# Deformable sampling and whitening on one core: an order of the stages by rounds, and a sampling step of short multiplies with one sum over the four corners

## The reference

```python
# layer 0, on n = group_norm(x, 32 groups)
offsets = conv3x3(n, offset_w) + offset_b          # 8 channels: (x, y) for 4 groups
mod     = 1 + tanh(conv3x3(n, mod_w) + mod_b)      # 4 channels
v       = conv1x1(n, kv_w)[256 value channels]     # 8 heads of 32
sampled = bilinear(v, pixel position + offsets) * mod   # 4 corners, weights times validity
x       = x + conv1x1(sampled, out_w) + out_b
# layer 1, on m = group_norm(x, 32 groups)
cov     = covariance of m over all images, in 16 groups of 16 channels, + 1e-4 I
x       = x + (cov ** -0.5) @ (m - mean) * weight + bias
```

## Time and profile before

| | us |
|---|---|
| median of three runs | 6920.73 |
| profiled execution, its own time | 6926.74 |
| its span, first to last instruction | 6925.0 |
| POOL busy | 4650.6 |
| PE busy | 4573.9 |
| DVE busy | 4258.7 |
| ACT busy | 1105.9 |
| mean granted TensorE clock | 0.833 |

### The profile page before, as it was taken

How to read it: one execution, slowest core, us unless ns; L and a number is a source line. 1 busy time by engine, 2 the same in 40 slices (tenths; PEclk the granted TensorE clock), 3 DMA queues, 4 the chain that set the end, 5 groups by cost and what they waited for, 6 DMA issues and landing times.

```text
span 6925.0 us, 71293 instructions
## 1 busy us (share of the span) xinstructions
PE 4573.9 (66%) x17916; PEld 2997.6 (43%) x17916; DVE 4258.7 (61%) x8374; ACT 1105.9 (16%) x2723; POOL 4650.6 (67%) x4115
## 2 busy tenths in 40 slices
PE   5866666666667666666666666666666544447777
PEld 3544444444444444444444444444444333334222
DVE  6766666666666666666666666666655544445555
ACT  1211112111211121112111121112111111110000
POOL 0277777777777777777777777777777777760000
PEclk9988888888888888888888888888888766668999
DMA  8966667666666667667676676676666544446999
GB/s 269 297 227 230 223 224 234 230 222 232 230 225 226 227 221 234 225 230 231 224 232 224 219 235 232 224 234 200 214 198 210 159 136 137 136 153 251 421 421 416
DMA packets 1069691, 1612.55 MB, mean 233 GB/s; under 512 B 92080, under 2 KB 617008, under 8 KB 1067568
## 3 DMA queue, kind: packets, MB, share of 16 engines
q0 software_dynamic: 196608, 537.13, 24.2%
q10 hardware_dynamic: 632832, 536.91, 23.1%
q1 hardware_dynamic: 240176, 537.77, 21.3%
HBM read 1074.58 MB, written 536.87 MB: 233 GB/s over the span
## 4 chain that ended last, share of the span: by engine, by line
POOL 66%; issue 19%; DMA 9%; PE 3%; DVE 2%; POOLq 0%; ACT 0%; DVEq 0%; ACTq 0%; SPq 0%
POOL patch L836 66%; DMA out_dram<-vring 4%; DMA vring<-x 3%; DMA v<-vring 1%; PE psT L1088 1%; PE psA L937 0%; DVE vring L782 0%; PE psG L1088 0%; PE psI L1088 0%; PE psO L937 0%; DVE bst L406 0%; PE psI L952 0%; PE psA L890 0%; DVE vring L472 0%; PE psT L894 0%
## 5 line engine op out<-in xcount | busy, mean ns | idle before, releaser
L836 POOL DMA_INDIRECT patch<-v,index_now x4096 | 4644.7, 1134 | 1537.4 <-issue 1536.8
L566 DVE TENSOR_TENSOR patch<-patch,weight 128x2048 f32<-128x2048 f32 x512 | 1173.0, 2291 | 1988.4 <-DMA patch<-v,index_now 1936.1
L937 PE MATMUL psA<-wB,xa_mem 128*128 128x364 f32 x3824 | 1525.0, 540 | 65.1 <-DVE taps L484 57.6
L990 PE MATMUL psT<-ident,xr 128*128 128x128 f32 x2048 | 462.9, 402 | 1519.6 <-DVE xr L582 1508.9
L990 PEld LDWEIGHTS psT<-ident,xr 128*128 128x128 f32 x2048 | 373.4, 210 | 1724.0 <-DVE xr L582 1703.8
L937 PEld LDWEIGHTS psA<-wB,xa_mem 128*128 128x128 f32 x3824 | 801.9, 226 | 449.4 <-issue 137.7
L976 PE MATMUL psO<-sampT,wO_sb 128*128 128x512 f32 x2048 | 928.8, 596 | 0.9 <-ACT sampT L1123 0.9
L1140 ACT ACTIVATE x1T<-psT 128x512 f32<-128x512 f32 x512 | 302.2, 597 | 3179.4 <-PE psT L990 3169.2
L965 PE MATMUL psT<-ident,samp 128*128 128x128 f32 x2048 | 387.4, 317 | 467.2 <-DVE samp L573 460.8
L568 DVE TENSOR_TENSOR patch<-patch 128x1024 f32<-128x1024 f32 x512 | 627.1, 1225 | 17.5
L1005 PE MATMUL psG<-x1T 128*128 128x129 f32 x4096 | 614.0, 314 | 10.1 <-ACT x1T L1140 10.1
(11 more groups left out here) (197 smaller groups left out, 2839.3 us busy)
## 6 DMA issues: line engine op xcount, KB each, us to landing
v<-vring ACTq DMA_DIRECT2D x256, 1024.0 KB, 6.8
xa_mem<-x_dram SPq DMA_DIRECT2D x256, 512.0 KB, 8.4
xr<-x_dram SPq DMA_DIRECT2D x256, 512.0 KB, 6.4
x<-xr ACTq DMA_DIRECT2D x256, 512.0 KB, 3.0
xs_mem<-x_dram SPq DMA_DIRECT2D x224, 512.0 KB, 7.7
patch<-v,index_now POOLq DMA_INDIRECT x4096, 4.2
patch<-x SPq DMA_DIRECT2D x64, 1024.0 KB, 12.3
out_dram<-patch ACTq DMA_DIRECT2D x64, 1024.0 KB, 19.9
```

Of the source, the lines that this page charges most:

```text
L566: eng.tensor_tensor(v4, v4, w4, ALU.mult).then_inc(weighted, 1)
L836: eng.indirect_dma_start(out=patch[n][:, t, :], out_offset=None, in_=v2_flat[k], in_offset=bass.IndirectOffsetOnAxis(ap=index_now[n][:, t: ...
L937: mm = eng.matmul(conv_bank[wide][r][:, 0:NA], xa[j][:, c, r * W:(r + 1) * W], wB[:, c, :], start=(c == 0), stop=(c == CC - 1))
L990: mm = eng.transpose(psT[h][:, at:at + P], xr[j][:, c, row * W:(row + 1) * W], ident[:, :])
```

## The change

In VectorE's `sample` the one multiply of 2048 elements becomes four multiplies of 512 elements each (`SHORT` is 2 of the 8 image-row and group columns of a half), with one semaphore increment behind the fourth; the two adds become one `tensor_reduce` over the four corners, with the corner index as innermost axis. The `halved` semaphore goes.

The order of the round changes on every engine. VectorE: two rows of `conv_out`, both halves of `sample`, statistics, the other two rows, `place`, then the residual of the block before and, once per pair, the Gram sum of the pair before. TensorE: in round t it turns the samples of block t-1 instead of t, all four rows at once, and takes x1's turn and the Gram product of block t-2 instead of t-1; the output convolution stays at t-1, and moves from the front of the round to its end. ScalarE follows: `x1_store` and `x1_out` are of block t-2, `samples_out` is of block t-1. SyncE issues the load of the residual's x behind the statistics' load. The Gram sums are opened and closed within one pair (j = 0 opens, j = 1 closes), so that `gram_tail`, `gram_out` and the addition of the two (L665) are gone. At an image's end each engine works off the blocks that are left.

The diff, cut to its core (the same moves in ScalarE's `pair`, in the loads and in the semaphores' counts are left out):

```diff
+SHORT = 2
...
-                w4 = weight[:, bass.ds(((i * 2 + j) * 2 + h) * (NH * 4), NH * 4)].unsqueeze(2)\
-                    .to_broadcast([P, NH * 4, CG])
-                eng.tensor_tensor(v4, v4, w4, ALU.mult).then_inc(weighted, 1)
+                for t in range(0, NH, SHORT):
+                    w4 = weight[:, bass.ds((((i * 2 + j) * 2 + h) * NH + t) * 4, SHORT * 4)]\
+                        .unsqueeze(2).to_broadcast([P, SHORT * 4, CG])
+                    part = v4[:, t * 4:(t + SHORT) * 4, :]
+                    times = eng.tensor_tensor(part, part, w4, ALU.mult)
+                times.then_inc(weighted, 1)
                 eng.wait_ge(weighted, half)
-                eng.tensor_tensor(mine[:, :, 0:ENT], mine[:, :, 0:ENT], mine[:, :, ENT:PATCH],
-                                  ALU.add).then_inc(halved, 1)
-                eng.wait_ge(halved, half)
                 if h == 0:
                     eng.wait_ge(psT_free[CC - 1], (b * PAIRS + i) * 4 + 2 * j + SAMP_FREE - 3)
-                eng.tensor_tensor(samp[j][:, 2 * h:2 * h + 2, :].rearrange("p r (g e) -> p (r g) e", g=G),
-                                  mine[:, :, 0:CG], mine[:, :, CG:ENT], ALU.add)\
+                eng.tensor_reduce(samp[j][:, 2 * h:2 * h + 2, :].rearrange("p r (t e) -> p (r t) e", t=G),
+                                  mine.rearrange("p t (k e) -> p t e k", e=CG), AX_X, ALU.add)\
                    .then_inc(sampled[j][h], 1)
...
 # VectorE, pair
                     for j in range(2):
+                        if ca is not None and not (prepare and j == 0):
+                            conv_out(ca, ci, 1 - m, j, (0, 1), g is None)
                         if g is not None:
                             sample(g, i, m, q, j, 0)
-                            if j == 1:
-                                residual(g, i, 0)
-                            elif not first:
-                                residual(g, i - 1, 1)
-                                gram_add(g, i - 1)
+                            sample(g, i, m, q, j, 1)
...
+                        if g is not None:
+                            if j == 1:
+                                residual(g, i, 0)
+                                if not first:
+                                    gram_add(g, i - 1)
+                            elif not first:
+                                residual(g, i - 1, 1)
+                        if prepare and j == 0:
+                            prep(ca)
+                            conv_out(ca, ci, 1 - m, j, range(ROWS), g is None)
...
-            eng.wait_ge(psG_free, B * NG + 1)
-            step(eng.tensor_tensor(gram[:, :, :, :], gram[:, :, :, :], gram_tail[:, :, :, :],
-                                   ALU.add))
+            eng.wait_ge(psG_free, B * PAIRS + 1)
...
 # TensorE, pair
-                            conv((0, 1))
-                            before(out_conv)
-                            before(turn_x1)
-                            conv((2,))
+                            alongside = not (prepare and j == 0)
+                            if alongside:
+                                conv((0, 1))
+                            twice_before(turn_x1)
+                            if alongside:
+                                conv((2,))
                             if a is not None and j == 1:
                                 offsets(a, i, m, s is not None)
-                            turn_samples(g, i, j, 0)
-                            conv((3,))
-                            turn_samples(g, i, j, 1)
-                            before(gram_block)
+                            if alongside:
+                                conv((3,))
+                            before(turn_samples)
+                            twice_before(gram_block)
+                            before(out_conv)
+                            if not alongside:
+                                prep(ca)
+                                conv(range(ROWS))
 
                 pairs(eng, pair)
                 if g is not None:
+                    turn_x1(g, PAIRS - 1, 0)
+                    turn_samples(g, PAIRS - 1, 1)
+                    gram_block(g, PAIRS - 1, 0)
                     out_conv(g, PAIRS - 1, 1)
                     turn_x1(g, PAIRS - 1, 1)
                     gram_block(g, PAIRS - 1, 1)
```

More of the change, by code:

```diff
@@ L228, in conv_of @@
             return (s, 0) if ends(i)[1] else (a, i + 1)
-        NG = PAIRS + 1
         def offsets_use(b, q, more):
@@ L623, in pair @@
                             take_stats(s, 0, 1)
[L624 to L633, removed]
                         if s is not None and not last:
                             take_stats(s, i + 1, j)
-                        if ca is not None:
+                        if ca is not None and not (prepare and j == 0):
                             conv_out(ca, ci, 1 - m, j, (2, 3), g is None)
@@ L956, in offsets, with turn_samples @@
                 mm.then_inc(psI_full, 1)
-            def turn_samples(b, i, j, h):
-                eng.wait_ge(sampled[j][h], b * PAIRS + i + 3)
+            def turn_samples(b, i, j):
+                for h in range(2):
+                    eng.wait_ge(sampled[j][h], b * PAIRS + i + 3)
                 for c in range(CC):
-                    if h == 0:
-                        eng.wait_ge(psT_free[c], (b * PAIRS + i) * 4 + 2 * j + SAMP_FREE)
-                    for r in (2 * h, 2 * h + 1):
+                    eng.wait_ge(psT_free[c], (b * PAIRS + i) * 4 + 2 * j + SAMP_FREE)
+                    for r in range(ROWS):
                         mm = eng.transpose(psT[c][:, r * W:(r + 1) * W],
                                            samp[j][:, r, c * P:(c + 1) * P], ident[:, :])
-                    if h == 1:
-                        mm.then_inc(psT_full[c], 1)
+                    mm.then_inc(psT_full[c], 1)
             def out_conv(b, i, j):
@@ L994, in gram_block @@
             def gram_block(b, i, j):
-                first, last = ends(i)[0] and j == 0, ends(i)[1] and j == 1
-                opens, closes = j == 1 or first, j == 0 or last
+                opens, closes = j == 0, j == 1
                 for h in range(2):
@@ L1000, in gram_block @@
                 if opens:
-                    eng.wait_ge(psG_free, b * NG + (1 if first else i + 2))
+                    eng.wait_ge(psG_free, b * PAIRS + i + 1)
                 for c in range(CC):
@@ L1028, in before, with twice_before @@
                                 part(g, i - 1, 1)
+                        def twice_before(part):
+                            if not first:
+                                part(g, i - 1, j)
                         if g is None:
@@ L1173, in pair @@
                             indices(a, 0, 0, j)
[L1174 to L1180, removed]
+                        if g is not None and not first:
+                            x1_store(g, i - 1, j)
                         if ca is not None and not (prepare and j == 0):
@@ L1183, in pair @@
                         if g is not None:
-                            samples_out(g, i, j)
+                            if not first:
+                                x1_out(g, i - 1, j)
+                            if j == 1:
+                                samples_out(g, i, 0)
+                            elif not first:
+                                samples_out(g, i - 1, 1)
                         if prepare and j == 0:
@@ L1200, in image @@
                 if g is not None:
+                    x1_store(g, PAIRS - 1, 0)
+                    x1_out(g, PAIRS - 1, 0)
+                    samples_out(g, PAIRS - 1, 1)
                     x1_store(g, PAIRS - 1, 1)
                     x1_out(g, PAIRS - 1, 1)
-                    gram_out(g)
             root(0)
```

24 lines of the change are left out of this document (6 added, 18 removed).

## The result

The changed kernel took 6466.6 us in the median of four runs (6463.1 to 6476.8), the kernel before 6920.9 beside it: a ratio of 0.935, 95% interval 0.934 to 0.937. It is 454 us faster; 635 were forecast. The time lies above the forecast's own range (6210 to 6415) and inside the full one (6210 to 6560). The profiled execution took 6476.8 us, 185 more than the 6292 of the forecast's sum.

What follows compares the result with a forecast made beforehand. POOL's gather stream was taken as the bound: 6926.74 - 638 (held gathers regained) + 3 (the ends) = 6292 us profiled, 6286 in the median. Own range 6210 to 6415, full range 6210 to 6560.

Steps and rivals of the forecast that it cites:

- The bound and the hold: POOL: gathers at 1.252 us each set the pace; each of 512 multiplies holds one gather, 1.50 us each, 766 in all.
- Rival D: On POOL: the gather's wait is not tied to the multiply's length, so the time stays at 6921 us; chance 0.02.
- the inference that stood behind it: The Trainium skill's inference that descriptor generation for a DMA is not stalled by `tensor_tensor`; the time would stay near 6920 us.
- The hold is let go between neighbours: Gathers get in between the four short multiplies; loss 0.25 us per half, 128 us instead of 766, POOL gains 638.
- Rival A: POOL gets in only behind the last of the four multiplies, +118 us of held gathers, 7042 us in all; chance 0.05.
- New half: 4.84 us, 0.56 more: DVE's sampling step: multiplies 2.52 us, reduction 2.29; 0.56 us more per half (bounds 0.56 to 2.7), 36 us per image.
- I cost it at nothing: The new order's waits between DVE and PE add nothing (bounds -0.3 to +4 us per round for DVE).
- rival C: The new order makes DVE and PE wait for each other, over 2.9 us per round; at 4 us, 6560; chance 0.11.
- Rival B: DVE's reduction costs a second cycle per element, 2.13 us more per half; DVE sets the pace, 6624 us; chance 0.05.
- The ring lets POOL run four blocks ahead, over 60 us: At an image's end DVE is late, but POOL can go four blocks ahead, over 60 us.
- The ends: Start unchanged; behind the last gather PE does one block more, +3 us (bounds 0 to +8).

Runs made afterwards that it cites:

- e8: The kernel before with the new sampling step alone (four short multiplies, one reduction over 256-byte steps), in the old order; 6293.7 us (ratio 0.909).
- e10: The changed kernel with the old sampling step (one multiply, two adds), so the new order alone; 6925.4 us (ratio 1.001).
- e7: The changed kernel with the reduction reading four adjacent elements, so it adds up others than the reference does; 6318.5 us (ratio 0.913).
- e11: The changed kernel with DVE's first two rows of conv_out moved back between the two halves of sample; 6349.7 us (ratio 0.917).
- e9: The kernel before, old order, with four short multiplies and short adds of 512 elements, no reduction; 6327.0 us (ratio 0.914).
- e12: The kernel before, old order, with four short multiplies and a reduction over elements 16 bytes apart (adds up others than the reference); 6322 us, measured once.
- e6: The changed kernel, new order, with four short multiplies and short adds of 512 elements in place of the reduction; 6325.8 us (ratio 0.915).
- e5: The changed kernel unchanged, as a control on a further chip; 8066 us against 7762 for the kernel before (ratio 1.038).

## Why the prediction was right in sign and short in size

**The bound and the hold: right.** POOL's stream at 1.252 us per gather, plus what multiplies hold, gives every POOL-bound run: e8 has its first gather at 302, then 5128 + 116 held, then 738, in sum 6284 against a span of 6282. e10, with the long multiply, holds 754 us. Rival D is refuted by each of these, and so is the inference that stood behind it.

**The hold is let go between neighbours: right in nearly every half.** Rival A would have lost 1.7 us per half. In the changed kernel 277 of 4096 gathers last over 1.0 us, and all but three of them under 1.5. Measured loss 0.16 us per half (83 / 512), 0.25 in e7 and 0.23 in e8, where 0.25 was taken. Why it is lowest in the changed kernel is not shown: in e11 DVE waits as little for gathers (217 us against 200), and the loss is 0.24.

Those three were held across several multiplies. This is one of them:

```profile
1140.37 2.50 DVE L570 TENSOR_TENSOR patch<-patch,weight 128x512 f32<-128x512 f32 x4
1140.96 2.73 POOL L834 DMA_INDIRECT patch<-v,index_now  x1 [0.30 <-issue]
```

The gather starts 0.59 us into the run, just before the first multiply ends, and ends 0.82 us behind the end of the fourth, so it was held across three of them, which is what rival A said of every half. In e8 13 gathers last 2.3 to 3.1 us and end in the same way, and cost 20 of its 116 us; e9 has 5 and e12 10, and e6, e7 and e11 have none. The multiplies' pitch, 0.60 us, is the same as in the other halves. What makes these halves different stays open.

**"New half: 4.84 us, 0.56 more": the step that failed.** The multiplies were as forecast (691 ns, a run of 2.53 us). The reduction was 3.68 us instead of 2.29, within the bounds that were given (0.56 to 2.7 more, measured 1.97), but the wrong end was taken. The row that decided it was a copy of 16 elements, which is too short to tell: over 2048 elements the same reading costs 1398 ns, 0.68 each, and of 16 times that, 11 ns, the copy showed nothing. On DVE it is 64 × 1.97 = 126 us per image instead of 36. The Trainium skill (SBUF — State Buffer, Door 1), whose rule on new 16-byte lines was set against that row, was nearer than the row: the trace has a penalty, though of 0.65 of the cycle of 1.04 ns per element, not a whole one. But the trace has it at steps of 16 bytes already (e12), four float32, and the same note gives 4 fp32 as how far one can stride for free.

**"I cost it at nothing" (the order by rounds): failed too, and only together with the other.** The forecast expected the residual to cover the wait for the first two rows. The timelines of DVE and of TensorE in the changed kernel show why it doesn't:

```profile
2716.69 0.41 DVE L474 TENSOR_TENSOR carry<-psA,biasB 128x256 f32<-128x256 f32 x1
2717.02 0.26 DVE L486 TENSOR_TENSOR taps<-psA,biasB 128x108 f32<-128x108 f32 x1
2717.19 1.39 DVE L584 SCALAR_TENSOR_TENSOR xr<-psO,bo_sb,xr 128x512 f32<-128x512 f32 x2
2718.68 0.43 DVE L474 TENSOR_TENSOR vring<-psA,biasB 128x256 f32<-128x256 f32 x1
2719.02 0.26 DVE L486 TENSOR_TENSOR taps<-psA,biasB 128x108 f32<-128x108 f32 x1
2721.10 0.42 DVE L474 TENSOR_TENSOR vring<-psA,biasB 128x256 f32<-128x256 f32 x1 [1.83 <-PE psA L935]
```
```profile
2716.82 4.24 PE L935 MATMUL psA<-wB,xa_mem 128*128 128x364 f32 x8 [4.40 <-DVE taps L486]
```

TensorE has been idle 4.40 us until DVE empties a bank, and its two rows then take 4.24 us, at a granted clock of 0.62 in that stretch; the same eight matmuls take 2.61 us in the kernel before at 3005.8, where the stretch's clock is 1.00. DVE, with one residual of 1.39 us in between, stands 1.83 us at the second row. So 43 us per middle image, 305 in all. The forecast's condition for rival C, 2.9 us of extra waiting per round, was not met (in an image of 693 us DVE is idle 84, 2.6 per round, against 46, 1.4 per round, before). It did not have to be: the reduction had used up the slack that this condition stood on. Rival B priced the reduction at 4.4 us and 6624, rival C the order at 6560; what happened is two thirds of B (1.40 us of its 2.13 per half) with a third of C (43 us of its 128 per image). Neither alone would have cost anything to speak of, as e7 (C without B, 6318) and e8 (B without C, 6294) show. The rivals were listed as alternatives, and their sum was not. The full range holds the measured time because its upper end was rival C's 6560, and C was priced at more than the order cost; that the two errors together stayed below it is luck.

**"The ring lets POOL run four blocks ahead, over 60 us": not enough.** The forecast let this cover DVE's lateness at an image's end. Nearly all of POOL's waits stand there: 199 of 218 us in the changed kernel, the longest 19.2 us, and all of the 21 us of e7 and of the 61 us of e11 lie ahead of an image's third and fourth block. In e8 there are none. How DVE's work at that turn could be shortened was not tried.

**The ends: near.** The tail grew by 4.5 us (3 forecast), in e7 by none. But e8 and e12, whose end is the old one, have 738 us as well, so the 4.5 us are not shown to be the block more. The first gather moved by 3 to 9 us in kernels of the new order, and by 1.7 to 3.5 in those of the old: nothing was forecast there, and it was not looked into.

## What to carry to other kernels

Where one engine's stream is held by another's instructions, cutting these short can pay at once: of 766 us held, 683 came back on that engine here. The second engine's slack is then a budget on which every other edit draws; price edits against what is left after the others, and work out rivals in pairs. A price per element has to come from a row with enough elements: 16 hide what 2048 show.

## What the runs showed of the hardware

- A multiply with two inputs in SBUF holds a gather from about 0.15 us after the multiply's start to its end (511 gathers of the kernel before last over 1.5 us). Between back-to-back multiplies (pitch 0.60 us) the hold is let go in nearly every half, and the waiting gather goes on; in 3 of 512 halves of the changed kernel and 13 of 512 of e8 it lasted to the fourth multiply's end. Reductions and statistics hold nothing: the longest gather of e7 takes 1.47 us (longest 3.05 before), with 512 reductions of 2.29 us beside them.
- `tensor_reduce` of 2048 float32 elements in groups of four: 2286 ns for adjacent elements, 3778 at 16-byte steps, 3653 to 3684 at 256-byte steps.
- The same kernel can take 8 to 12% longer elsewhere: the kernel before took 6920 to 6927 us on three of the five of this study and 7515 and 7762 us on the two others, and the ratio of the two kernels went from 0.935 to 1.038. On the slow ones TensorE's semaphore updates appear late, 13.7 us behind the instruction's end in the event told under e5. Whether it is the chip or the time of the run is not shown. A change should be compared on chips on which the kernel before takes the same time.
